# Adding the attention mask on VectorE and moving the softmax's subtraction to GpSimd in a two-layer transformer kernel

## Chip, cores and metric

The kernel runs on one core of a Trainium2 chip. The metric is the device time of the whole program in microseconds (us), the median of the runs. The engines are TensorE (PE, with its weight loads shown apart as PEld), VectorE (DVE), ScalarE (ACT), GpSimd (POOL) and SyncE (SP, which issues most DMAs). Each has a queue of its own that runs in order, and they wait for each other through semaphores.

## What is computed

Two layers, each of an attention part and a block part with modulation around them. The change is in the block part, `local_attention`, which is there twice: six blocks with 16 heads and a window of 32 in the first layer, two blocks with 8 heads and a window of 64 in the second; 4096 rows of 128 features in both. Cut to what matters:

```python
def local_attention(q, k, v):            # window w, keys of this window and the one before
    bk2, bv2 = look(bk), look(bv)
    mask = (it < jb) | (it > jb + w) | (jb == -1)
    sim = jnp.einsum('bhwie,bhwje->bhwij', bq, bk2) * QK_SCALE
    sim = jnp.where(mask, -jnp.finfo(sim.dtype).max, sim)
    attn = jax.nn.softmax(sim, -1)
    return jnp.einsum('bhwij,bhwje->bhwie', attn, bv2)
```

Around it stand the projection to q, k and v, an l2 norm with scales and rotary tables on q and k, the output projection, and a feed-forward part with a layer norm and a Gelu gate.

## The kernel before

`two_layer_kernel` runs a row of stages one after the other. The change touches `local_block_stage` alone, which is called twice: as `L0` (6 blocks, 16 heads, window 32), from about 1040 to 4560 us of the profiled span, and as `L1` (2 blocks, 8 heads, window 64), from about 4900 us to the end.

A stage takes the rows in tiles of 128, 16 tiles to a sequence of 2048 rows, two sequences to a block. A counter `k` goes over block and sequence (`HL` = 12 passes in L0, 4 in L1), `T` over the 16 tiles. Each tile is worked in two halves, `hf` 0 and 1, each with half of the heads. Everything is pipelined by hand: in step (T, hf) each engine's `emit` works on items that lag by a fixed number of halves: projection 4, values and normed keys 6, scores 7 (`AT_SCORE`), softmax 8 (`AT_SOFTMAX`), weighted values 9 (`AT_PV`), output transposes 10. In the feed-forward part two tiles form a group: even T does the up projection (`TO_UP`) in hf 0 and the layer norm's work (`TO_LN`), odd T the feature transposes and the down projection in hf 0. Thus four kinds of half alternate: up half (hf 0, even T), even output half (hf 1, even T), down half (hf 0, odd T), odd output half (hf 1, odd T). DVE, ACT, POOL and SP unroll 16 tiles per loop turn (`bodies`); PE unrolls two tiles (`paired_bodies`), with a tile number that is partly in a register (`Tile`).

The order in each queue is that of `emit`:

- PE: query/key projection (L1437), transposes of q and k (L1472), transposes of the attended values (L1491), values (L1506), transposes of the probabilities (L1521), then up projections (L1612), or output (L1533) and input transpose (L1543), or feature transposes and down projection (L1597, L1624); then the scores: two bf16 mask products against an identity (L1556) that open the PSUM banks, and the score products (L1564) that add to them; last the weighted values (L1585 in L0, L1587 in L1). The Gelu's gate shares PSUM banks with the weighted values, so they wait for `hidden_done` in the up half.
- DVE: reciprocal (L1855) and scaling (L1860) of the weighted values, `shift`: the negated maximum of the scores (L1869) and its addition to them (L1874), both read from PSUM; then the rotation (L1889, L1890) with the sum of squares (L1891), `clamp` (L1900), `add_output` (L1908), or `gated` (L1939) and `deviations`, or `add_group` (L1950).
- ACT: squares (L1677), copies of the q/k transposes (L1688), output copy (L1696), in hf 0 `roots` (L1704, L1707); in the up half exponentials (L1729), value copy (L1722), probability copy (L1737), table load (L1791), Gelus (L1795), table load; in the other halves value copy, then (even output half) `normalised` (L1773), exponentials, probability copy. `affine` (L1785) ends the down half.
- POOL: in hf 0 `refine`, four small steps that wait for ACT's root (L1977 to L1983); in the even output half `deviation_refine`, seven small steps (L2021 to L2033); then `to_unit_length` (L1993), in hf 1 `scaled_table` (L2012), and `add_parts` (L2002).

The buffer `probs` takes the shifted scores; ACT's exponential works in place on it.

Of the kernel before, what the change touches and what calls it, by code (L numbers as in the profile page):

```python
# [13 lines left out]
ALU = mybir.AluOpType  # L14
# [1025 lines left out]
def local_block_stage(nc, name, depth, heads, window, x, x_rows, mid_rows, v_rows, weights, tables):  # L1040
# [18 lines left out]
    with ExitStack() as ctx:  # L1059
# [28 lines left out]
        probs = sb("probs", [128, 2, 512])  # L1088
        neg_max = sb("neg_max", [128, 2, 2 * HU])
# [47 lines left out]
            "ss_done", "rotated", "max_done", "shifted", "rec_done", "att_done", "clamped", "mid_done", "bn_stats", "bn_eps", "bn_aggr", "var_done",  # L1137
# [124 lines left out]
        with nc.Block() as block:  # L1262
# [161 lines left out]
            def _(pe):  # L1424
# [84 lines left out]
                def prob_transposes(k, T, hf):  # L1509

                    t, h = item(T, hf, AT_PV)
                    if live(k, t):
                        pe.wait_ge(v2_in[parity(t)][h], turns(k, t, 16 * V2_LOADS))
# [31 lines left out]
                def of_sequence(t):  # L1545

                    return ds((t.turn * 2 + t.step % NP) % NP, 1) if isinstance(t, Tile) else slice(t % NP, t % NP + 1)

                def scores(k, T, hf):

                    t, h = item(T, hf, AT_SCORE)
                    if live(k, t):
                        wait(pe, S["shifted"], halves(k, t, h - 1))
                        wait(pe, S["kprev_done"], count(k, t, 1, 0))
                        for p in range(2):
                            nc.tensor.matmul(S_VIEW[:, p, :, :], ident_bf[:, :], masks[:, of_sequence(t), :].to_broadcast([128, HU, 2 * W]), start=True, stop=False)  # L1556
                        pe.wait_ge(consts_in, CONSTS)
                        pe.wait_ge(S["qkT_done"], steps_(k, t, NS * h + NS - 1))
                        kk = 1 + parity(t)
                        for i in range(HU):  # L1560
                            for a in range(NB):
                                for p in range(2):
                                    rows, u = slice(64 * p, 64 * p + 64), HU * h + i
                                    last = nc.tensor.matmul(S_VIEW[W * a:W * a + W, p, i, :], qkT[rows, 0, u, W + W * a:2 * W + W * a],  # L1564
                                                            qkT[rows, kk, u, W * a:W * a + 2 * W], start=False, stop=(i == HU - 1))
# [270 lines left out]
            def _(dve):  # L1836
# [25 lines left out]
                def shift(k, T, hf):  # L1862

                    t, h = item(T, hf, AT_SOFTMAX)
                    if live(k, t):
                        wait(dve, S["shifted"], halves(k, t - 1, h))
                        dve.wait_ge(S["score_ps"], halves(k, t, h))
                        top = neg_max[:, h, :].rearrange("x (p u) -> x p u", p=2)
                        nc.vector.tensor_reduce(top, S_VIEW, AX.X, ALU.max, negate=True).then_inc(S["max_done"], 1)  # L1869
                        wait(dve, S["pT_ps"], halves(k, t - 1, h))  # L1870
                        dve.wait_ge(S["max_done"], halves(k, t, h))
                        dst = probs[:, h, :].rearrange("x (u p k) -> x p u k", u=HU, p=2)
# [96 lines left out]
            def _(pool):  # L1969
# [65 lines left out]
                def emit(k, T, hf):  # L2035
                    if hf == 0:
                        refine(k, T)
                    elif T % 2 == TO_LN % 2:
                        deviation_refine(k, T)
# [107 lines left out]
```

## Time and profile before

| | us |
|---|---|
| median of 3 runs | 5893.61 |
| range of the runs | 5891.54 to 5894.18 |
| profiled execution | 5897.42 |
| its span | 5895.6 |

| engine | busy us | share of the span |
|---|---|---|
| PE | 4715.3 | 80% |
| PE weight loads | 3408.2 | 58% |
| DVE | 4302.1 | 73% |
| ACT | 3151.1 | 53% |
| POOL | 2961.3 | 50% |

The granted TensorE clock is full (1.00) over both block stages apart from their ends; its mean over the span is 0.886. How to read it: the shares are means over stages of different kinds. In the two block stages each engine repeats the same order of instructions every two tiles, so one such turn, read in order of time, stands for the stage. A row of the timeline has the start, the duration, the engine, the line, the operation with output and input, and in brackets how long the engine was idle before it and what released it.

### The profile page before, as it was taken

The numbers are of one execution on the slowest core, as the hardware profiler recorded it, in microseconds if no ns is written. First come the engines' busy times: TensorE is split into PE (matmuls) and PEld (weight loads), VectorE is DVE, ScalarE is ACT, GpSimd is POOL, SyncE is SP. The second block draws the span as 40 slices with busy tenths as digits, with TensorE's granted clock in tenths as the row PEclk, the third lists the DMA queues.
The fourth block names the chain that finished last, engine by engine and source line by source line (L and its number), as shares of the span: only waits on it lengthen the run. The fifth ranks groups of instructions, "written<-read, shape, count | busy, mean of one in ns | idle before, by whom it ended". The sixth has DMA issues, their size and how long they took to land. (4 is left out here: it accounts for less than half of the span.)

```text
span 5895.6 us, 217646 instructions
## 1 busy us (share of the span) xinstructions
PE 4715.3 (80%) x78080; PEld 3408.2 (58%) x78080; DVE 4302.1 (73%) x9236; ACT 3151.1 (53%) x6761; POOL 2961.3 (50%) x4044
## 2 busy tenths in 40 slices
PE   2005675799999999999999999999993774888886
PEld 1004553566666666666666666666663553666665
DVE  5995677677777777777777777777775545766665
ACT  1000221466666666666666666666662121666665
POOL 0886000566666666666666666666661001545442
PEclk6555666899999999999999999999997556999998
DMA  1000000445444454455454545454541001333332
GB/s 65 0 0 1 25 21 26 127 125 131 132 129 132 128 135 127 131 130 135 124 138 124 134 127 135 123 138 122 137 125 39 0 0 50 108 109 106 104 109 76
DMA packets 708756, 564.14 MB, mean 96 GB/s; under 512 B 227460, under 2 KB 633704, under 8 KB 707848
## 3 DMA queue, kind: packets, MB, share of 16 engines
q1 hardware_dynamic: 694920, 537.26, 34.3%
q10 hardware_dynamic: 13312, 22.02, 1.2%
q14 instruction: 455, 3.73, 0.2%
q8 instruction: 69, 1.13, 0.1%
HBM read 359.55 MB, written 199.76 MB: 95 GB/s over the span
## 5 line engine op out<-in xcount | busy, mean ns | idle before, releaser
L2002 POOL TENSOR_TENSOR L_qk<-L_cos_part,L_sin_part 128x512 f32<-128x512 f32 x896 | 1128.7, 1274 | 187.0 <-DVE L_sin_part L1890 186.5
L1677 ACT ACTIVATE L_squares<-L_ps_q 128x512 f32<-128x512 f32 x896 | 535.0, 597 | 1074.1 <-PE L_ps_q L1437 1064.3
L1437 PE MATMUL L_ps_q<-L_w_qkv,L_xT 128*128 128x512 f32 x1792 | 975.1, 626 | 67.8 <-issue 51.4
L1993 POOL TENSOR_TENSOR L_qk<-L_qk,L_rnorm 128x1024 f32<-128x1024 f32 (+1 forms) x512 | 865.1, 1690 | 20.7 <-POOL L_rnorm L1983 1.1
L1472 PEld LDWEIGHTS L_ps_t<-L_ident,L_qk 128*128 128x128 f32 x3584 | 448.0, 141 | 478.3 <-issue 375.6
L1889 DVE TENSOR_TENSOR L_cos_part<-L_ps_q,L_rot 128x512 f32<-128x512 f32 x896 | 609.4, 680 | 46.2 <-POOL L_rot L2012 34.7
L1977 POOL TENSOR_TENSOR L_nw_a<-L_rnorm 128x32 f32<-128x32 f32 (+1 forms) x256 | 60.0, 234 | 1116.4 <-ACT L_rnorm L1707 1116.2
L1890 DVE TENSOR_TENSOR L_sin_part<-L_ps_q,L_rot 128x512 f32<-128x512 f32 x896 | 609.2, 680 | 0.0
L1891 DVE TENSOR_REDUCE L_sumsq<-L_squares 128x8 f32<-128x512 f32 x896 | 604.8, 675 | 0.0
L1472 PE MATMUL L_ps_t<-L_ident,L_qk 128*128 128x128 f32 x3584 | 540.6, 274 | 3.7 <-POOL L_qk L1993 3.6
L1506 PE MATMUL L_ps_t<-L_w_qkv,L_xT 128*128 128x512 f32 (+1 forms) x1024 | 479.9, 550 | 74.6 <-issue 72.9
L1688 ACT ACTIVATE L_qkT<-L_ps_t 128x512 f32<-128x512 f32 x896 | 530.0, 592 | 14.1 <-PE L_ps_t L1472 13.8
L1533 PE MATMUL L_ps_q<-L_w_out,L_outT 128*128 128x128 f32 x3584 | 443.7, 276 | 1.7 <-ACT L_outT L1696 1.7
L2012 POOL TENSOR_TENSOR L_rot<-L_rot_base,L_qk_scales 128x256 f32<-128x256 f32 x256 | 187.6, 733 | 509.8 <-DMA L_qk_scales<-in_L_ffn_k_scale 508.8
L1533 PEld LDWEIGHTS L_ps_q<-L_w_out,L_outT 128*128 128x128 f32 x3584 | 421.5, 192 | 2.3 <-issue 2.3
L1521 PEld LDWEIGHTS L_ps_t<-L_ident,L_probs 128*128 128x128 f32 x2048 | 224.1, 140 | 333.8 <-issue 258.0
L1564 PE MATMUL L_ps_s<-L_qkT 64*32 64x64 f32 (+1 forms) x26624 | 416.1, 229 | 0.0
L1874 DVE TENSOR_TENSOR L_probs<-L_ps_s,L_neg_max 128x512 f32<-128x512 f32 x512 | 354.1, 692 | 53.5 <-DVE L_neg_max L1869 0.5
L1855 DVE RECIPROCAL L_p_rec<-L_ps_o 128x8 f32<-128x8 f32 (+1 forms) x512 | 103.0, 201 | 392.7 <-PE L_ps_o L1585 265.4
L1564 PEld LDWEIGHTS L_ps_s<-L_qkT 64*32 64x32 f32 (+1 forms) x26624 | 322.9, 107 | 108.1 <-issue 108.1
L1585 PE MATMUL L_ps_o<-L_val,L_probsT 64*32 64x65 f32 x24576 | 330.7, 226 | 61.2 <-DVE L_hidden L1939 50.7
L1860 DVE TENSOR_TENSOR L_att<-L_ps_o,L_p_rec 128x512 f32<-128x512 f32 (+1 forms) x512 | 320.0, 625 | 60.7 <-DVE L_p_rec L1855 10.8
(295 smaller groups left out, 9734.4 us busy)
## 6 DMA issues: line engine op xcount, KB each, us to landing
L_val<-v_rows SPq DMA_DIRECT2D x896, 260.0 KB, 3.9
v_rows<-L_val SPq DMA_DIRECT2D x384, 260.0 KB, 2.3
v_rows<-L_val SPq DMA_DIRECT2D x512, 65.0 KB, 2.2
L_rot_base<-in_rot SPq DMA_DIRECT2D x256, 128.0 KB, 2.1
v_rows<-L_val SPq DMA_DIRECT2D x128, 130.0 KB, 2.1
L_x_in<-x_rows SPq DMA_DIRECT2D x512, 32.0 KB, 1.7
mid_rows<-z SPq DMA_DIRECT2D x256, 64.0 KB, 1.6
L_f_in<-mid_rows SPq DMA_DIRECT2D x256, 64.0 KB, 2.0
```

Source lines behind the costliest of these rows:

```text
L1437: nc.tensor.matmul(ps_q[j % 2][:, :], xT[:, parity(t), :], w_qkv[:, 0:2, 256 * j:256 * j + 256], start=True, stop=True).then_inc(S["proj_p ...
L1472: last = nc.tensor.transpose(ps_t[0][:, 128 * i:128 * i + 128], qk[:, parity(t), h, s, 128 * i:128 * i + 128], ident[:, :])
L1506: nc.tensor.matmul(ps_v[:, 0:128 * HU], xT[:, parity(t), :], w_qkv[:, 2, 128 * HU * h:128 * HU * h + 128 * HU], start=True, stop=True).the ...
L1533: last = nc.tensor.matmul(ps_q[0][:, 0:128], outT[:, u, :], w_out[:, u, :], start=(u == 0), stop=(u == U - 1))
L1564: last = nc.tensor.matmul(S_VIEW[W * a:W * a + W, p, i, :], qkT[rows, 0, u, W + W * a:2 * W + W * a], qkT[rows, kk, u, W * a:W * a + 2 * W ...
L1677: nc.scalar.activation(squares[:, j % 2, :], ps_q[j % 2][:, :], ACT.Square).then_inc(S["sq_done"], 1)
L1688: nc.scalar.activation(dst, ps_t[0][:, :].rearrange("x (a u q) -> x a u q", a=2, u=2), ACT.Copy).then_inc(S["qkT_done"], 1)
L1889: nc.vector.tensor_tensor(R4(cos_part[:, j % 2, :]), qkp, cs[:, :, 0, :, :, :].to_broadcast([128, 2, 4, 2, 32]), ALU.mult)
L1890: nc.vector.tensor_tensor(R4(sin_part[:, j % 2, :]), qkp[:, :, :, ::-1, :], cs[:, :, 1, :, :, :].to_broadcast([128, 2, 4, 2, 32]), ALU.mul ...
L1891: nc.vector.tensor_reduce(sumsq[:, t % 2, j, :], squares[:, j % 2, :].rearrange("x (g d) -> x g d", g=8), AX.X, ALU.add).then_inc(S["ss_do ...
L1993: nc.gpsimd.tensor_tensor(v, v, r, ALU.mult).then_inc(S["normed"], 1)
L2002: nc.gpsimd.tensor_tensor(qk[:, t % 2, h, s, :], cos_part[:, j % 2, :], sin_part[:, j % 2, :], ALU.add).then_inc(S["added"], 1)
```

## The change

The two mask products on PE go. Each score product now opens and closes its own accumulation. DVE's `shift` becomes `mask`: it adds the mask (bf16, broadcast over heads) to the scores while it reads them from PSUM, and writes to a new SBUF tile `masked`; the maximum is then taken from `masked`. The subtraction of the maximum moves to POOL, in a new `shift` that reads `masked` and writes `probs`; it stands in POOL's queue behind `refine` or `deviation_refine` and ahead of `to_unit_length`. DVE's `mask` waits for POOL's previous `shift`. PE no longer waits for `shifted` and for `kprev_done` ahead of the scores; in the loop, the wait for the buffer stands ahead of the probability transposes (`masked`).

```diff
@@ sb
         probs = sb("probs", [128, 2, 512])
+        masked = sb("masked", [128, 512])
@@ PE, prob_transposes
                     if live(k, t):
+                        if isinstance(T, Tile):
+                            last_scores, g = item(T, hf, AT_SOFTMAX)
+                            pe.wait_ge(S["masked"], halves(k, last_scores, g))
@@ PE, scores
-                        wait(pe, S["shifted"], halves(k, t, h - 1))
-                        wait(pe, S["kprev_done"], count(k, t, 1, 0))
-                        for p in range(2):
-                            nc.tensor.matmul(S_VIEW[:, p, :, :], ident_bf[:, :], masks[:, of_sequence(t), :].to_broadcast([128, HU, 2 * W]), start=True, stop=False)
+                        before, keys = halves(k, t, h - 1), steps_(k, t, NS * h + NS - 1)
                         pe.wait_ge(consts_in, CONSTS)
-                        pe.wait_ge(S["qkT_done"], steps_(k, t, NS * h + NS - 1))
+                        if not isinstance(T, Tile):
+                            wait(pe, S["masked"], before)
+                        pe.wait_ge(S["qkT_done"], keys)
...
-                                                            qkT[rows, kk, u, W * a:W * a + 2 * W], start=False, stop=(i == HU - 1))
+                                                            qkT[rows, kk, u, W * a:W * a + 2 * W], start=True, stop=True)
@@ DVE
-                def shift(k, T, hf):
+                def mask(k, T, hf):
 
                     t, h = item(T, hf, AT_SOFTMAX)
                     if live(k, t):
-                        wait(dve, S["shifted"], halves(k, t - 1, h))
+                        wait(dve, S["shifted"], halves(k, t, h - 1))
                         dve.wait_ge(S["score_ps"], halves(k, t, h))
-                        top = neg_max[:, h, :].rearrange("x (p u) -> x p u", p=2)
-                        nc.vector.tensor_reduce(top, S_VIEW, AX.X, ALU.max, negate=True).then_inc(S["max_done"], 1)
-                        wait(dve, S["pT_ps"], halves(k, t - 1, h))
-                        dve.wait_ge(S["max_done"], halves(k, t, h))
-                        dst = probs[:, h, :].rearrange("x (u p k) -> x p u k", u=HU, p=2)
-                        wide = neg_max[:, h, :].rearrange("x (p u o) -> x p u o", p=2, o=1).to_broadcast([128, 2, HU, 2 * W])
-                        nc.vector.tensor_tensor(dst, S_VIEW, wide, ALU.add).then_inc(S["shifted"], 1)
+                        allowed = masks[:, t % NP, :].rearrange("x (p u k) -> x p u k", p=1, u=1).to_broadcast([128, 2, HU, 2 * W])
+                        view = masked[:, :].rearrange("x (u p k) -> x p u k", u=HU, p=2)
+                        nc.vector.tensor_tensor(view, S_VIEW, allowed, ALU.add).then_inc(S["masked"], 1)
+                        dve.wait_ge(S["masked"], halves(k, t, h))
+                        top = neg_max[:, h, :].rearrange("x (u p) -> x u p", p=2)
+                        nc.vector.tensor_reduce(top, masked[:, :].rearrange("x (u p k) -> x u p k", u=HU, p=2), AX.X, ALU.max, negate=True).then_inc(S["max_done"], 1)
@@ POOL
+                def shift(k, T, hf):
+
+                    t, h = item(T, hf, AT_SOFTMAX)
+                    if live(k, t):
+                        wait(pool, S["pT_ps"], halves(k, t - 1, h))
+                        pool.wait_ge(S["max_done"], halves(k, t, h))
+                        wide = neg_max[:, h, :].rearrange("x (n o) -> x n o", o=1).to_broadcast([128, 2 * HU, 2 * W])
+                        nc.gpsimd.tensor_tensor(probs[:, h, :].rearrange("x (n k) -> x n k", k=2 * W), masked[:, :].rearrange("x (n k) -> x n k", k=2 * W), wide, ALU.add).then_inc(S["shifted"], 1)
@@ POOL, emit
                         deviation_refine(k, T)
+                    shift(k, T, hf)
                     to_unit_length(k, T, hf)
```

## Rows read from the trace of the kernel before

**Rows 1.** The page, busy us, share of the span and instructions of each engine.

```profile
PE 4715.3 (80%) x78080; PEld 3408.2 (58%) x78080; DVE 4302.1 (73%) x9236; ACT 3151.1 (53%) x6761; POOL 2961.3 (50%) x4044
```

**Rows 2.** The timeline, first stage's up half: start, duration, engine, line, tiles.

```profile
2911.61 0.69 DVE L1874 TENSOR_TENSOR L_probs<-L_ps_s,L_neg_max 128x512 f32<-128x512 f32 x1
2914.30 0.63 ACT L1729 ACTIVATE L_probs<-L_probs 128x512 f32<-128x512 f32 x1
2914.48 0.25 POOL L1983 TENSOR_TENSOR L_rnorm<-L_rnorm,L_nw_a 128x32 f32<-128x32 f32 x1
2914.81 1.90 POOL L1993 TENSOR_TENSOR L_qk<-L_qk,L_rnorm 128x1024 f32<-128x1024 f32 x1
2915.31 0.60 ACT L1737 ACTIVATE L_probsT<-L_ps_t 128x512 f32<-128x512 f32 x1
2915.93 1.28 ACT L1791 ACT_TABLE_LOAD   x1
2918.78 0.47 DVE L1939 SCALAR_TENSOR_TENSOR L_hidden<-L_ps_o,L_b_up,L_gate 85x256 f32<-85x256 f32 x1
2919.32 0.72 PEld L1585 LDWEIGHTS L_ps_o<-L_val,L_probsT 64*32 64x32 f32 x64 [0.69 <-issue]
```

**Rows 3.** The timeline, first stage's even output half.

```profile
2922.39 0.20 POOL L2033 TENSOR_TENSOR L_f_b<-L_f_b,L_minus_one 128x2 f32<-128x2 f32 x1
2925.63 0.62 ACT L1729 ACTIVATE L_probs<-L_probs 128x512 f32<-128x512 f32 x1
...
2926.32 1.28 POOL L2002 TENSOR_TENSOR L_qk<-L_cos_part,L_sin_part 128x512 f32<-128x512 f32 x1
2926.41 1.24 DVE L1900 TENSOR_TENSOR L_nw_x<-L_sumsq,L_tiny 128x32 f32<-128x32 f32 x1
2926.60 0.38 PE L1556 MATMUL L_ps_s<-L_masks,L_ident_bf 128*128 x2
2926.91 0.70 PEld L1564 LDWEIGHTS L_ps_s<-L_qkT 64*32 64x32 f32 x64 [0.21 <-issue]
2928.53 0.21 DVE L1855 RECIPROCAL L_p_rec<-L_ps_o 128x8 f32<-128x8 f32 x1 [0.68 <-PE L_ps_o L1585]
```

**Rows 4.** Groups by line, second stage: count, busy us, mean ns, idle before.

```profile
L2002 POOL TENSOR_TENSOR L_qk<-L_cos_part,L_sin_part 128x512 f32<-128x512 f32 x128 | 162.7, 1271 | 63.1 <-DVE L_sin_part L1890 63.1
L1993 POOL TENSOR_TENSOR L_qk<-L_qk,L_rnorm 128x512 f32<-128x512 f32 x128 | 133.6, 1044 | 5.7 <-POOL L_rnorm L1983 1.1
L1874 DVE TENSOR_TENSOR L_probs<-L_ps_s,L_neg_max 128x512 f32<-128x512 f32 x128 | 88.5, 692 | 13.6 <-DVE L_neg_max L1869 0.5
L1891 DVE TENSOR_REDUCE L_sumsq<-L_squares 128x8 f32<-128x512 f32 x128 | 86.4, 675 | 0.0
```

**Rows 5.** The timeline, second stage's up half.

```profile
5304.78 0.61 ACT L1729 ACTIVATE L_probs<-L_probs 128x512 f32<-128x512 f32 x1
5305.85 0.22 POOL L1983 TENSOR_TENSOR L_rnorm<-L_rnorm,L_nw_a 128x16 f32<-128x16 f32 x1
```

**Rows 6.** The timeline, first stage's down half.

```profile
2932.52 0.25 POOL L1983 TENSOR_TENSOR L_rnorm<-L_rnorm,L_nw_a 128x32 f32<-128x32 f32 x1
2933.12 0.62 ACT L1729 ACTIVATE L_probs<-L_probs 128x512 f32<-128x512 f32 x1
2933.64 0.59 ACT L1737 ACTIVATE L_probsT<-L_ps_t 128x512 f32<-128x512 f32 x1
2935.83 0.72 PEld L1585 LDWEIGHTS L_ps_o<-L_val,L_probsT 64*32 64x32 f32 x64
```

**Rows 7.** The timeline, second stage's down half.

```profile
5319.59 0.62 ACT L1729 ACTIVATE L_probs<-L_probs 128x512 f32<-128x512 f32 x1
5320.03 0.22 POOL L1983 TENSOR_TENSOR L_rnorm<-L_rnorm,L_nw_a 128x16 f32<-128x16 f32 x1
5320.11 0.59 ACT L1737 ACTIVATE L_probsT<-L_ps_t 128x512 f32<-128x512 f32 x1
5322.27 0.60 PEld L1587 LDWEIGHTS L_ps_o<-L_val,L_probsT 128*64 128x64 f32 x16 [0.17 <-issue]
```

**Rows 8.** Line L1900's own view: count, ns min/median/max, first and last start.

```profile
L1900 DVE TENSOR_TENSOR L_nw_x<-L_sumsq,L_tiny x256: 174/674/1324, 1058.8 to 5818.1; 128x32 f32<-128x32 f32 x96, 128x16 f32<-128x16 f32 x32
```

More of the change, by code:

```diff
@@ L1135, in local_block_stage @@
             "ln_log", "ln_root", "fnorm_done", "fT_done", "gelu_done",
-            "ss_done", "rotated", "max_done", "shifted", "rec_done", "att_done", "clamped", "mid_done", "bn_stats", "bn_eps", "bn_aggr", "var_done",
+            "ss_done", "rotated", "masked", "max_done", "shifted", "rec_done", "att_done", "clamped", "mid_done", "bn_stats", "bn_eps", "bn_aggr", "var_done",
             "hidden_done", "new_done",
@@ L1543, in input_transpose @@
                         nc.tensor.transpose(ps_v[:, 0:128], x_in[:, parity(t), :], ident[:, :]).then_inc(S["xT_ps"], 1)
-                def of_sequence(t):
-                    return ds((t.turn * 2 + t.step % NP) % NP, 1) if isinstance(t, Tile) else slice(t % NP, t % NP + 1)
                 def scores(k, T, hf):
@@ L1953, in emit @@
                     normalise(k, T, hf)
-                    shift(k, T, hf)
+                    mask(k, T, hf)
                     for s in range(NS):
```

## Prediction, made before the changed kernel was seen

> **What bounds the kernel now.** I read the page first. PE is busy for 80% of the span, DVE 73%, ACT 53%, POOL 50% [rows 1]: in a mean over all stages PE leads, and POOL looks as if it had room. But a share of the span says nothing of which wait ends last, so I went to the order of time in the middle of each block stage, half by half. A half is one call of each engine's `emit`; I measure from the end of one weighted-values product (L1585, L1587) to the end of the next. Four kinds alternate: the up half (hf 0, even T: up projections, Gelu), the even output half, the down half (hf 0, odd T: down projection), the odd output half. Two tiles are one turn of four halves: 12 x 8 = 96 turns in the first block stage, 4 x 8 = 32 in the second.
>
> In three kinds of half of the first stage PE sets the length: after the transposes of the probabilities it runs without a gap up to the weighted values. The mask product lies in that gapless stretch [rows 3]. The up half is different. There ACT works from the exponentials through the copy of the values, the copy of the transposed probabilities, the table load and the three Gelus with no gap; DVE's `hidden` follows, and PE's weighted values, whose PSUM bank the gate shares, start at 2919.32, behind `hidden` which ended at 2919.25; PE's weight loads stood idle for 0.69 us just before [rows 2]. The table load starts 2915.93, the exponentials stood at 2914.30. In this half ACT is the limit, and what ACT's queue waits for is what counts.
>
> **Mask products removed.** PE streams the mask from 2926.60, the product's row has 0.38 us, and the scores start at 2926.91, after 0.21 us of idle weight loads [rows 3]. Without the product the scores can start at 2926.60: 0.31 us for a half. The bounds are 0.21 (only that idle goes) and 0.38 (the whole row). The saving counts only where PE sets the half.
>
> **DVE.** Before: a maximum from PSUM and a subtraction from PSUM. After: an addition that reads PSUM and the bf16 mask, and a maximum from SBUF. The addition has the form of L1874, one operand from PSUM and one broadcast, 692 ns; the SBUF reduce has that of L1891, 675 ns [rows 4]. So DVE has the same load, and the maximum is done about when the subtraction is done now: its 0.68 us starts where L1874 starts, at 2911.61, so it ends at about 2912.29 in the up half [rows 2]. Nothing of DVE is on the path for that.
>
> **The subtraction on POOL: its price.** 512 elements with one broadcast operand on POOL: L1993 in the second stage is just that, 1044 ns. L2002, with two full operands, takes 1271 ns [rows 4]; that is the upper end, and I take 1.04 because the access patterns agree. It occurs 512 times, 535 us, which brings POOL from 50% to some 59%: no bound by load.
>
> The Trainium skill (GPSIMD Engine Reference, "Engine selection") advises against moving two-input elementwise work there and calls it about twice as slow as on VectorE. Twice 692 ns would be an estimate of 1.38 us; by it the forecast below would be 54 us higher (0.34 us in 160 halves). This trace's row for the same shape gives a factor of 1.5, and the sum goes by the row.
>
> **Its place in POOL's queue.** This decides. `shift` is emitted after `refine` (hf 0) or `deviation_refine`, and ahead of `to_unit_length`. In hf 0 `refine` waits for ACT's root of the same half, so the subtraction, whose input has been there since 2912.29, waits for a chain that it has nothing to do with. ACT's exponentials then wait for POOL, and behind them in ACT's queue stand, in the up half, the value copy, the probability copy, the table load and the Gelus. Everything now gapless moves.
>
> Up half, first stage: the chain's last operation ends at 2914.73 and POOL's next one starts at 2914.81; in that place the subtraction runs to 2915.85. A step from engine to engine costs 0.07 (`hidden` ends at 2919.25, PE follows at 2919.32), so ACT starts at 2915.92, where it starts at 2914.30 now [rows 2]. That is 1.62 us later, and `hidden` and the weighted values move by as much, since the stretch behind is rigid. The 0.31 saved on PE vanishes in a longer wait. Second stage: the chain ends at 5306.07, the subtraction at 5307.19, the exponentials start at 5307.26 instead of 5304.78: 2.48 us [rows 5].
>
> Down half, first stage: the chain ends at 2932.77, exponentials at 2933.96 instead of 2933.12, so 0.84 later; the probability copy ends at 2935.07 instead of 2934.23. The weighted values would start at 2935.83 - 0.31 = 2935.52 [rows 6]: 0.45 us to spare, and the 0.31 is kept. In the second stage this cover is too thin: chain end 5320.25, exponentials 5321.44 instead of 5319.59, 1.85 later; the probability copy then ends at 5322.55, the weighted values start at 5322.62 instead of 5322.27 [rows 7]: 0.35 us lost, nothing saved.
>
> Output halves: no `refine` there. In the even one POOL's seven small steps end at 2922.59 and the maximum at 2922.69, so the subtraction is done near 2923.8, and ACT comes to these exponentials only at 2925.63 [rows 3]: hidden, 0.31 kept. The odd one is the same in the first stage. In the second the late down half pushes DVE's sum and with it the maximum back; I let that half keep nothing, and bound it by 0.31 kept or lost.
>
> What else queues behind the subtraction on POOL: `to_unit_length` (PE's transposes of it come one half later), `scaled_table` and `add_parts` (DVE's rotation of the next half wants their buffers, behind four other DVE instructions). They move by 1 to 2 us, which I cost at nothing. No DMA is moved; the value stores of the up half leave later by what ACT's copy is late, and their readers come three halves on. PE's new wait for `masked` ahead of the probability transposes is met over 1 us early.
>
> **One cost of another kind.** DVE's `clamp` (L1900) takes the larger of two SBUF tiles. It took 1.24 us where POOL's L2002 was running beside it, the two ending at 2927.65 and 2927.60 [rows 3]; over the kernel it took 174 ns at least and 1324 at most [rows 8]. With POOL fuller it will wait nearly always. In this even output half DVE still idles 0.68 us before its next reciprocal [rows 3], so I cost it at nothing; if it misses a further POOL instruction, see the second rival. The rule behind it is in the Trainium skill (SBUF — State Buffer, "Who interferes with whom"): a DVE instruction with two SBUF inputs and a GpSimd instruction that reads SBUF exclude each other for a whole instruction. By that rule, the trace agrees (174 against 1324 ns), and the new mask addition, with one operand in PSUM, is free of it.
>
> **The sum.** First stage: 96 x 1.62 = +155.5 for up halves; 96 x 3 x 0.31 = -89.3 for the others. Second: 32 x (2.48 + 0.35 - 0.31 + 0) = +80.6. Together +146.8 us. The profiled execution took 5897.4 us, its span 5895.6, the median of the runs is 5893.6; all lie within 0.1%, so the sum is set on the median: 5893.6 + 146.8 = 6040 us, 2.5% slower. Bounds: POOL at 1.27 adds 0.23 x 160 = 37; the mask at 0.21 or 0.38 moves 320 halves, +32 or -22; the odd output half of the second stage, 10 either way.
>
> **Rivals.** (a) Faster than before: ACT's order turns out to have slack in the up half, because `refine` ends earlier once the kernel has settled, or the Gelus wait for PE's gate product and not for ACT. Then the up halves cost nothing and only the 320 savings and the second stage's 0.35 stand: 5893.6 - 99 + 11 = 5805 us. It decides where the subtraction ends before 2914.3. Against it: the table load starts 0.03 us after the copy, with no idle time [rows 2]. Chance 5%.
> (b) DVE becomes late through `clamp`: one further L2002, 1.27 us, in the even output half. `clamp` would end at 2928.92 with the sum `z` still behind it, and the next reciprocal, today at 2928.53, is wanted at 2928.22: about 1 us in each of 128 turns, +128: 6168 us. It is for the case that POOL's back-to-back instructions keep DVE out; against it, at 2926.41 DVE waited for one instruction only [rows 3]. Chance 8%.
> (c) The mask product was hidden beside the issue of the scores, the saving is nothing: 5893.6 + 155.5 + 32 x 2.83 = 6140. Chance 5%.
> (d) Part of the delay is given back later (ACT's idle time ahead of the next half's squares lets PE and ACT re-form), half of 236 us: about 5922. Chance 7%, of which a third within 0.2% or below.
>
> The forecast's mechanism holds 75%. The range 5975 to 6115 takes in the bounds and leaves out most of the rivals, about 2 in 10. A measurement of this kernel can tell 0.2% (12 us) from no change. Chances: faster 6%, same 2%, slower 92%.
>
> **What would show it.** Up halves longer by 1.6 and 2.5 us, POOL's new line between L1983's and L1993's counterparts there, ACT's exponentials idle before it with POOL as the releaser, some 1.5 us in the first stage's up halves and 0.8 in its down halves; PE's wait for `hidden` grown; output halves 0.3 us shorter; granted clock still full in these stages. It is wrong if the exponentials never wait for POOL, if POOL's line costs well over 1.27 us, or if `clamp` delays the next half.

## The result, and the profile after

The changed kernel takes 6035.86 us (median of 4 runs, 6029.47 to 6041.25) against 5893.9 us before (4 runs, 5891.54 to 5895.73): a ratio of 1.0241, with a 95% interval of 1.0223 to 1.0258. It is 142 us slower. The profiled execution took 6036.01 us, its span 6034.2 us.

First the page of the changed kernel: the busy time of the engines, and three of its groups (busy us, mean ns of one, idle time before and what ended it).

```profile
PE 4639.1 (77%) x77056; PEld 3313.0 (55%) x77056; DVE 4361.9 (72%) x9236; ACT 3157.4 (52%) x6761; POOL 3456.1 (57%) x4556
...
L1990 POOL TENSOR_TENSOR L_probs<-L_masked,L_neg_max 128x512 f32<-128x512 f32 x512 | 533.1, 1041 | 196.4 <-DVE L_neg_max L1872 191.5
...
L1728 ACT ACTIVATE L_probs<-L_probs 128x512 f32<-128x512 f32 x512 | 320.2, 625 | 316.7 <-POOL L_probs L1990 316.6
...
L1937 DVE SCALAR_TENSOR_TENSOR L_hidden<-L_ps_t,L_b_up,L_gate 128x256 f32<-128x256 f32 x256 | 112.1, 479 | 460.3 <-ACT L_gate L1794 439.1
```

PE has lost 76 us of work, POOL has gained 495 [rows 1], and neither is what the time went by. The second and third groups are: ACT was idle for 317 us ahead of the exponentials, all but 0.1 us of it released by POOL's subtraction, and DVE for 439 us behind the Gelus. By the medians of the wait (1.34 us in the first stage's up halves, 2.22 in the second's), some 200 of the 317 us stand in the up half; most of the rest stands in the down halves (0.58 and 1.58 us). The timeline of the changed kernel, first stage: the weighted values that end the odd output half, then the up half up to its own weighted values.

```profile
2972.53 0.85 PE L1584 MATMUL L_ps_o<-L_val,L_probsT 64*32 64x65 f32 x64
...
2975.12 0.69 DVE L1872 TENSOR_REDUCE L_neg_max<-L_masked 128x8 f32<-128x512 f32 x1
...
2978.05 0.25 POOL L1981 TENSOR_TENSOR L_rnorm<-L_rnorm,L_nw_a 128x32 f32<-128x32 f32 x1
...
2978.26 1.04 POOL L1990 TENSOR_TENSOR L_probs<-L_masked,L_neg_max 128x512 f32<-128x512 f32 x1
...
2979.34 0.63 ACT L1728 ACTIVATE L_probs<-L_probs 128x512 f32<-128x512 f32 x1 [1.34 <-POOL L_probs L1990]
...
2980.96 1.28 ACT L1790 ACT_TABLE_LOAD   x1
...
2980.99 1.13 PE L1611 MATMUL L_ps_t<-L_f_normT,L_w_up 128*128 128x256 f32 x4 [0.49 <-ACT L_probsT L1736]
...
2982.76 0.87 DVE L1937 SCALAR_TENSOR_TENSOR L_hidden<-L_ps_t,L_b_up,L_gate 128x256 f32<-128x256 f32 x2 [3.34 <-ACT L_gate L1794]
...
2984.13 0.85 PE L1584 MATMUL L_ps_o<-L_val,L_probsT 64*32 64x65 f32 x64 [1.22 <-DVE L_hidden L1937]
```

These rows answer to [rows 2]. The maximum is there at 2975.81, POOL takes the subtraction up at 2978.26, behind the last step of the chain, ACT's exponentials start 5.96 us after the previous weighted values ended (2979.34 - 2973.38) where they started at 4.50 before (2914.30 - 2909.80), and the half is 11.60 us long. A second engine feels the delay: PE's last up products (L1611) wait 0.49 us for ACT's copy of the probabilities, which they did not do before. They end at 2982.12, though, and `hidden` starts only at 2982.76, behind the first Gelu, so the Gelus still set the half's end. The next half, the even output half, of the same timeline; it answers to [rows 3]:

```profile
2991.22 1.24 DVE L1898 TENSOR_TENSOR L_nw_x<-L_sumsq,L_tiny 128x32 f32<-128x32 f32 x1
...
2991.48 0.70 PEld L1563 LDWEIGHTS L_ps_s<-L_qkT 64*32 64x32 f32 x64 [0.17 <-issue]
...
2992.14 0.85 PE L1584 MATMUL L_ps_o<-L_val,L_probsT 64*32 64x65 f32 x64
...
2993.09 0.21 DVE L1854 RECIPROCAL L_p_rec<-L_ps_o 128x8 f32<-128x8 f32 x1 [0.44 <-PE L_ps_o L1584]
```

It is 8.01 us long. Weight loads still stand idle for 0.17 us ahead of the scores, and DVE still has idle time behind its clamp. The second stage, up half and even output half:

```profile
5516.39 0.71 PE L1586 MATMUL L_ps_o<-L_val,L_probsT 128*64 128x65 f32 x16
...
5521.33 1.04 POOL L1990 TENSOR_TENSOR L_probs<-L_masked,L_neg_max 128x512 f32<-128x512 f32 x1
5522.40 0.63 ACT L1728 ACTIVATE L_probs<-L_probs 128x512 f32<-128x512 f32 x1 [2.22 <-POOL L_probs L1990]
...
5526.98 0.70 PE L1586 MATMUL L_ps_o<-L_val,L_probsT 128*64 128x65 f32 x16 [1.41 <-issue]
...
5532.92 0.70 PE L1586 MATMUL L_ps_o<-L_val,L_probsT 128*64 128x65 f32 x16 [0.25 <-issue]
```

Here ACT waits 2.22 us for POOL, and the up half takes 10.58 us (5527.68 - 5517.10).

One turn says little of the others, so I took from the timeline of each kernel all halves of both stages and the median length of each kind, from the end of one weighted-values product to the end of the next (90 to 93 halves of each kind in the first stage, 25 or 26 in the second; the others miss a record). The runs of the next section stand in the same table. U is the up half, N the even output half, F the down half, O the odd output half; a "turn" is the sum of the four means.

| kernel | U, N, F, O, first stage | turn | U, N, F, O, second stage | turn |
|---|---|---|---|---|
| before | 10.41, 8.22, 8.31, 8.24 | 35.28 | 8.44, 5.94, 6.75, 5.87 | 27.24 |
| after | 11.61, 8.00, 8.08, 8.15 | 36.04 | 10.53, 5.94, 6.95, 5.65 | 29.39 |
| e1_shift_first | 10.40, 8.00, 8.08, 8.13 | 34.70 | 8.64, 5.94, 6.54, 5.65 | 27.12 |
| e2_shift_late | 13.91, 8.00, 9.43, 8.22 | 40.11 | 12.12, 7.25, 8.06, 5.65 | 33.09 |
| e5b_act_plus3 | 10.43, 8.24, 8.30, 8.24 | 35.35 | 8.46, 5.94, 6.75, 5.87 | 27.29 |
| e7_before_exp_last | 10.41, 8.22, 8.32, 8.24 | 35.24 | 8.44, 5.94, 6.75, 5.87 | 27.28 |
| e3_exp_last | 10.40, 8.00, 8.08, 8.15 | 34.72 | 8.45, 5.94, 6.94, 5.66 | 27.30 |
| e6_both | 10.40, 8.00, 8.08, 8.15 | 34.72 | 8.44, 5.94, 6.54, 5.65 | 26.87 |
| e4_products_back | 11.62, 8.22, 8.30, 8.35 | 36.59 | 10.48, 5.94, 6.94, 5.86 | 29.55 |
| e9_all_dve | 10.41, 9.64, 8.08, 8.66 | 37.03 | 8.45, 5.93, 6.87, 5.66 | 27.42 |

From before to after the turns grow by 0.76 and 2.15 us: 96 x 0.76 + 32 x 2.15 = 142 us. That this is the measured difference to the microsecond is partly luck: for other kernels of the table the same sum is off by up to some 14 us. A direct count needs no mean. From the first to the last start of DVE's maximum (L1869 before, L1872 after) the first stage took 3388.3 us before and 3447.1 after, the second 846.0 and 927.1: 59 and 81 us more. Together that is 140 us, and the span grew by 139. Nothing is lost outside the two block stages, but the second has lost more than its turns show. The difference stands at its start. The first twelve halves, in which the feed-forward part hasn't set in and a half is short, took 66.2 us before and 84.5 after. First one such half of the changed kernel, then those twelve halves by the windows view, before and after (us of the window, busy and count of PE, PEld, DVE, ACT and POOL, granted clock, DMA share, GB/s):

```profile
5083.15 0.63 ACT L1728 ACTIVATE L_probs<-L_probs 128x512 f32<-128x512 f32 x1 [2.22 <-POOL L_probs L1990]
...
5084.64 0.71 PE L1586 MATMUL L_ps_o<-L_val,L_probsT 128*64 128x65 f32 x16 [2.53 <-issue]
```

```profile
4992.60:5058.80 66.20, 58.16 (x602) 40.56 (x603) 48.88 (x100) 39.43 (x98) 37.94 (x61) 0.98 0.43 116
```

```profile
5051.30:5135.80 84.50, 65.69 (x583) 44.91 (x582) 49.36 (x99) 40.48 (x99) 49.66 (x73) 0.85 0.36 95
```

Each of the six halves with hf 0 waits 1.5 to 2.2 us for POOL's subtraction there, PE stands still ahead of the weighted values (2.53 us in the row), and the granted clock of the stretch is 0.85 where it was 0.98, so PE was on the lower of its two levels for a part of it.

### The profile page after: what moved, and what is told of

It reads as the page before. It is cut to its first block and busy times, and to the rows that moved or that the text cites. A ratio compares the mean times of both kernels' runs of the same rounds, so it can differ in the third digit from the quotient of the medians.

```text
span 6034.2 us, 215298 instructions
## 1 busy us (share of the span) xinstructions
PE 4639.1 (77%) x77056; PEld 3313.0 (55%) x77056; DVE 4361.9 (72%) x9236; ACT 3157.4 (52%) x6761; POOL 3456.1 (57%) x4556
## 5 line engine op out<-in xcount | busy, mean ns | idle before, releaser
L2000 POOL TENSOR_TENSOR L_qk<-L_qk,L_rnorm 128x1024 f32<-128x1024 f32 (+1 forms) x512 | 863.9, 1687 | 0.2
L1990 POOL TENSOR_TENSOR L_probs<-L_masked,L_neg_max 128x512 f32<-128x512 f32 x512 | 533.1, 1041 | 196.4 <-DVE L_neg_max L1872 191.5
L1728 ACT ACTIVATE L_probs<-L_probs 128x512 f32<-128x512 f32 x512 | 320.2, 625 | 316.7 <-POOL L_probs L1990 316.6
L1937 DVE SCALAR_TENSOR_TENSOR L_hidden<-L_ps_t,L_b_up,L_gate 128x256 f32<-128x256 f32 x256 | 112.1, 479 | 460.3 <-ACT L_gate L1794 439.1
```

The costliest lines, as they stand in the source:

```text
L1990: nc.gpsimd.tensor_tensor(probs[:, h, :].rearrange("x (n k) -> x n k", k=2 * W), masked[:, :].rearrange("x (n k) -> x n k", k=2 * W), wide ...
L2000: nc.gpsimd.tensor_tensor(v, v, r, ALU.mult).then_inc(S["normed"], 1)
```

## The experiments

Two theories stood at the start. Mine: the loss is the subtraction's place in POOL's queue, behind a chain that waits for ACT, and it reaches the end through ACT's exponentials in the up half. The rival: the loss is the subtraction on POOL as such, a fuller engine, wherever it is put. Then, since the up half lost less than ACT was delayed, the question was how much slack it had; then, what the mask products had cost PE; and last, whether POOL was needed at all.

### The subtraction ahead of the chain

`e1_shift_first` is the changed kernel with one call moved in POOL's queue:

```diff
                 if hf == 0:
+                    shift(k, T, hf)
                     refine(k, T)
-                elif T % 2 == TO_LN % 2:
-                    deviation_refine(k, T)
-                shift(k, T, hf)
+                else:
+                    if T % 2 == TO_LN % 2:
+                        deviation_refine(k, T)
+                    shift(k, T, hf)
                 to_unit_length(k, T, hf)
```

> The changed kernel with one edit: in the halves with hf 0, POOL emits the subtraction ahead of refine instead of behind it; the other halves are as they were. Theory (the late exponentials are the whole loss): in the first stage's up half the maximum is done 2.43 us after the half's start, so the subtraction ends near 3.57 and the exponentials start where they did before the change (4.51); the up half falls from 11.61 to 10.41 us, the down half stays; 96 x 1.20 = 115 us back. In the second stage the exponentials start near 3.3 instead of 5.24, the up half falls by about 1.97 us, the down half by 0.3: 32 x 2.3 = 74 us back. About 5847 us, faster than the kernel before. Rival (POOL's added load, or clamp's waits for POOL, are the loss): the work on POOL is the same, so 6036 us within 15.

Measured: 5840.93 us (4 runs), 0.9909 of before, interval 0.9892 to 0.9925. The same instructions on the same engines, in another order on one of them, are 195 us faster than the changed kernel and 53 us faster than the one before. Its timeline, an up half of the first stage (the previous weighted values ended at 3020.09, 10.41 us before these do):

```profile
3022.60 1.04 POOL L1990 TENSOR_TENSOR L_probs<-L_masked,L_neg_max 128x512 f32<-128x512 f32 x1 [2.03 <-DVE L_neg_max L1872]
...
3024.60 0.63 ACT L1728 ACTIVATE L_probs<-L_probs 128x512 f32<-128x512 f32 x1
3024.77 0.25 POOL L1981 TENSOR_TENSOR L_rnorm<-L_rnorm,L_nw_a 128x32 f32<-128x32 f32 x1
...
3028.28 0.88 DVE L1937 SCALAR_TENSOR_TENSOR L_hidden<-L_ps_t,L_b_up,L_gate 128x256 f32<-128x256 f32 x2 [2.14 <-PE L_ps_t L1611]
...
3029.65 0.85 PE L1584 MATMUL L_ps_o<-L_val,L_probsT 64*32 64x65 f32 x64 [0.77 <-DVE L_hidden L1937]
```

POOL had been idle for 2.03 us when the maximum came; the subtraction is over before the chain's last step, and ACT's exponentials show no wait. The up half is back at 10.40 us. POOL's load is as in the changed kernel (3476.0 us busy against 3456.1), so the load costs next to nothing and the place nearly all. In the second stage the up half keeps 0.20 us (8.64): ACT is ready for the exponentials at 2.88 us in the median (from the previous weighted values), and the subtraction ends at 3.32. The slow start of the second stage is gone too: its first twelve halves take 66.6 us.

### The subtraction later still

`e2_shift_late`, again the changed kernel:

```diff
-                shift(k, T, hf)
                 to_unit_length(k, T, hf)
+                shift(k, T, hf)
```

> The changed kernel with one edit: POOL emits the subtraction behind to_unit_length in every half. This doubles the suspected wait. Theory (the late exponentials): they move by the 1.90 us (first stage) or 1.04 us (second) of to_unit_length. First stage: up half +1.9, down half +1.2 (the probability copy then ends after the scores), output halves 0: 96 x 3.1 = 298 us. Second stage: up and down halves +1.0 each, output halves +0.7 and +0.9: 32 x 3.6 = 116. About 6450 us. Rival (load of POOL or clamp): the order does not matter, 6036 us within 15.

Measured: 6536.35 us, one run, so without an interval. The rival fell once more: the work on POOL is the same, and the kernel is 500 us slower than the changed one. U grows to 13.91 and F to 9.43, in the second stage all but O. Counted as above, from the first to the last maximum, the first stage is 384 us longer than in the changed kernel where 298 was expected, the second 111 for 116: the 86 us above the expectation stand in the first stage. They are taken up at the end, with what the clock did.

### How much slack the up half had

In the changed kernel the exponentials of the first stage start 1.45 us later (median 5.96 after the previous weighted values, 4.51 before), yet the up half grew by 1.20. The group of `hidden` shows where 0.25 went. First the changed kernel, then the kernel before, from the groups by line in the window 1030 to 4600 us, the first stage (idle us before the group, and what ended it):

```profile
L1937 DVE SCALAR_TENSOR_TENSOR L_hidden<-L_ps_t,L_b_up,L_gate 128x256 f32<-128x256 f32 x192 | 84.1, 479 | 320.5 <-ACT L_gate L1794 308.9 <-PE L_ps_t L1611 11.6
```

```profile
L1939 DVE SCALAR_TENSOR_TENSOR L_hidden<-L_ps_t,L_b_up,L_gate 128x256 f32<-128x256 f32 x192 | 84.1, 480 | 195.6 <-PE L_ps_t L1612 172.1 <-ACT L_gate L1795 23.4
```

Before the change `hidden` waited for PE's up projection, not for ACT's Gelu. ACT's work was gapless in [rows 2], but the half went by PE. Two kernels without the change test that. `e7_before_exp_last` sends the exponentials behind the Gelus, to take them out of ACT's path:

```diff
                     if hf == 0 and T % 2 == TO_UP % 2:
-                        exponentials(k, T, hf)
                         val_copy(k, T, hf)
                         prob_copy(k, T, hf)
                         gates(k, T)
+                        exponentials(k, T, hf)
```

> The kernel before the change with one edit: in up halves ScalarE does the exponentials behind the Gelus and the second table load instead of ahead of the value copy. That takes 0.55 us out of the chain that the prediction called the limit of the up half. By the prediction (ScalarE is the limit there) 128 x 0.55 = 70 us faster, 5824. By the trace after (VectorE's first hidden product waited for PE's up products, 0.25 us later than for the Gelu) the up half stays: 5894 within 10.

Measured: 5894.97 us (10 runs), 0.9998, interval 0.9989 to 1.0008: no change, as the trace of after had it. Its timeline, up half of the first stage:

```profile
3017.69 0.60 ACT L1722 ACTIVATE L_val<-L_ps_t 128x512 f32<-128x512 f32 x1 [0.61 <-PE L_ps_t L1506]
...
3020.65 0.87 DVE L1939 SCALAR_TENSOR_TENSOR L_hidden<-L_ps_t,L_b_up,L_gate 128x256 f32<-128x256 f32 x2 [2.10 <-ACT L_gate L1795]
...
3022.01 0.85 PE L1585 MATMUL L_ps_o<-L_val,L_probsT 64*32 64x65 f32 x64 [0.55 <-DVE L_hidden L1939]
3022.59 0.63 ACT L1729 ACTIVATE L_probs<-L_probs 128x512 f32<-128x512 f32 x1
```

With the exponentials gone, ACT idles for 0.61 us until PE has the values ready: they had filled a gap. The median start of the Gelus moves from 7.44 to 7.35 only, and `hidden` does not move at all (8.19). So the edit didn't take 0.55 us out of ACT's path but 0.09, and as a test it is weaker than its expectation has it: if ACT were the limit, it would have given some 10 us, not 70. Against 10 us the measured interval (-6 to 5 us) says a little, and `hidden` standing still says more. That this row names a Gelu as the releaser is no proof against it: the second of the three Gelus ends at 7.35 + 2 x 0.40 = 8.15, just ahead of `hidden`, but `hidden` doesn't need it, for in the kernel before it starts at 8.19 with the second Gelu running to 8.24. The name is that of the event that came last. The other side, and the stronger test, is `e5b_act_plus3`, also from the kernel before, with three small copies added to ACT's queue (cut: the line that declares `spare`):

```diff
                     if hf == 0 and T % 2 == TO_UP % 2:
+                        for _i in range(3):
+                            nc.scalar.activation(spare[:, 2 * _i:2 * _i + 2], minus_half[:, :], ACT.Copy)
                         exponentials(k, T, hf)
```

> The kernel before the change with three small ScalarE copies (128x2, about 0.20 us each) ahead of the exponentials in the up halves. By the prediction's reading (in the up half ACT is the limit, no slack) 128 x 0.6 = 77 us: 5971. By the trace after, ScalarE's chain had 0.25 us of slack, because VectorE's first hidden product waited for PE's up products and not for the Gelu: 128 x 0.35 = 45 us: 5939.

Measured: 5907.09 us (10 runs), 1.002, interval 1.001 to 1.003. Both expectations were far too high, for one reason that has nothing to do with the question: the copies cost the queue 0.28 us, not the 0.6 I had taken. Its timeline:

```profile
3022.19 0.39 ACT L1810 ACTIVATE L_spare<-L_minus_half 128x2 f32<-128x2 f32 x3
3022.47 0.63 ACT L1730 ACTIVATE L_probs<-L_probs 128x512 f32<-128x512 f32 x1
```

and its group of `hidden` in the first stage:

```profile
L1942 DVE SCALAR_TENSOR_TENSOR L_hidden<-L_ps_t,L_b_up,L_gate 128x256 f32<-128x256 f32 x192 | 84.1, 479 | 205.8 <-ACT L_gate L1796 199.1 <-PE L_ps_t L1613 6.8
```

The exponentials start 0.28 us later (median 4.79), the Gelus 0.27 (7.71), `hidden` 0.03 (8.22), and its releaser is now the Gelu. So the slack was 0.25 us: of 0.28, 0.03 came through, and of 1.45 in the changed kernel, 1.20. By the turns' means (35.28 to 35.35, 27.24 to 27.29) the cost is 96 x 0.07 + 32 x 0.05 = 8 us, inside the measured interval of 6 to 18. Had ACT been the limit with no slack, the same 0.28 us would have cost 128 x 0.28 = 36 us, which that interval excludes.

### The exponentials out of the way

If the loss goes through ACT's exponentials, it can also be mended there, with POOL's queue left as the change has it. `e3_exp_last` is the changed kernel with the edit of `e7_before_exp_last`.

> The changed kernel with the same edit on ScalarE (exponentials last in up halves), POOL's order untouched. POOL's subtraction stays as late as it was, but nothing that the half's end needs queues behind the exponentials. Theory: the first stage's up half falls from 11.61 to 10.41 us, the second's from 10.53 to 8.44, the down halves keep their loss: 96 x 1.20 + 32 x 2.09 = 182 us back, 5854. If the loss came from POOL's load or from clamp: 6036 within 15.

Measured: 5857.14 us (4 runs), 0.9932, interval 0.9916 to 0.9949; the up halves are back at 10.40 and 8.45. An edit that is worth nothing in the kernel before is worth 179 us here. Against `e1_shift_first` 16 us are left: the down half of the second stage (6.94 against 6.54), whose exponentials the edit doesn't touch, and 10 us at the start of the second stage, whose first twelve halves take 76.3 us against 66.6. `e6_both` has both edits.

> Both cures in one kernel: POOL's subtraction ahead of refine in hf 0, and ScalarE's exponentials last in up halves. Against the first cure alone (5841) only the second stage's up half has something left to gain, 8.64 to 8.44 us, 32 x 0.2 = 6 us: 5835. Should the up half be limited by ScalarE, 128 x 0.5 more would go: 5775.

Measured: 5827.17 us (4 runs), 0.9882, interval 0.9866 to 0.9899. It is the fastest kernel of the study, 1.2% faster than the one before. It is also 14 us below `e1_shift_first`, where 6 were expected and the turns give 6; what the other 8 are was not looked into. The 5775 of the expectation proves nothing either way, since in `e7_before_exp_last` the edit moved the Gelus by 0.09 us and not by 0.5. Against before, by medians, it keeps the three savings on PE in the first stage and two in the second: 96 x (0.22 + 0.23 + 0.09) + 32 x (0.21 + 0.22) = 66 us, of 68 measured.

### The mask products put back

`e4_products_back` is the changed kernel with PE's two products in their old place, the DVE's addition kept:

```diff
+                        for p in range(2):
+                            nc.tensor.matmul(S_VIEW[:, p, :, :], ident_bf[:, :], masks[:, of_sequence(t), :].to_broadcast([128, HU, 2 * W]), start=True, stop=False)
...
-                                                            ..., start=True, stop=True)
+                                                            ..., start=False, stop=(i == HU - 1))
```

> The changed kernel with the two bf16 mask products put back on PE ahead of the scores, DVE's addition kept (the mask is added twice, which changes no weight). It prices the products alone. By the trace after, the scores start 0.22 us earlier without them in the first stage's output and down halves and the half gets shorter by 0.09 to 0.23; put back they should cost 96 x (0.22 + 0.23 + 0.15) + 32 x 0.2 = 64 us: about 6100 us. By the prediction's 0.31 us in 288 + 32 halves it would be 99 us, 6135. If the products are hidden (rival c), 6036 within 10.

Measured: 6106.04 us (4 runs), 1.0357, interval 1.034 to 1.0375: 70 us above the changed kernel. An even output half of its timeline:

```profile
3030.14 0.21 PEld L1562 LDWEIGHTS L_ps_s<-L_masks,L_ident_bf 128*128 128x128 bf16 x2
3030.24 0.38 PE L1562 MATMUL L_ps_s<-L_masks,L_ident_bf 128*128 x2
3030.55 0.70 PEld L1570 LDWEIGHTS L_ps_s<-L_qkT 64*32 64x32 f32 x64 [0.21 <-issue]
```

The rows look just as in [rows 3], product to scores 0.31 us; but the halves grow by 0.22 (N), 0.22 (F) and 0.20 (O), and by 0.21 in the second stage's O. The up half doesn't grow, nor does the second stage's N. 96 x 0.64 + 32 x 0.21 = 68 us. Without the product the weight loads stand idle for 0.17 us ahead of the scores anyway, so of the 0.31 between the two starts a part is not the product's.

### The subtraction back on DVE

The subtraction costs DVE 0.69 us, and the idle time ahead of `hidden` seemed to have room for it. `e9_all_dve` does it there, from `masked`, behind the maximum; POOL's queue is as before the change.

```diff
# DVE, mask(), behind the maximum; POOL's shift is removed
+                        wait(dve, S["pT_ps"], halves(k, t - 1, h))
+                        dve.wait_ge(S["max_done"], halves(k, t, h))
+                        nc.vector.tensor_tensor(probs[:, h, :]..., masked[:, :]..., wide, ALU.add).then_inc(S["shifted"], 1)
```

> The changed kernel with the subtraction on VectorE, reading masked and the maxima from SBUF; PE without mask products as in the change; POOL as before the change. VectorE has one more instruction of some 0.7 us in each half, with two SBUF inputs, so it may also wait for POOL. Theory: the exponentials come at 3.2 us or so, in time for every half, so no loss of the change's kind; but VectorE's stretch to its last instruction in the output halves grows from 7.6 to 8.3 us and passes the half's 8.0: +0.3 us in the first stage's 192 output halves against the first cure, about 5841 + 58 = 5900. If VectorE's load has room after all: 5841.

Measured: 6067.79 us (4 runs), 1.0296, interval 1.0279 to 1.0313. Neither came true. The timeline of an even output half of the first stage, then the line's own view (count, ns min, median, max):

```profile
3002.65 1.90 POOL L1995 TENSOR_TENSOR L_qk<-L_qk,L_rnorm 128x1024 f32<-128x1024 f32 x1
3002.85 2.25 DVE L1876 TENSOR_TENSOR L_probs<-L_masked,L_neg_max 128x512 f32<-128x512 f32 x1
...
3004.51 1.17 POOL L2014 TENSOR_TENSOR L_rot<-L_rot_base,L_qk_scales 128x256 f32<-128x256 f32 x1
...
3006.35 1.86 PEld L1537 LDWEIGHTS L_ps_q<-L_w_out,L_outT 128*128 128x128 f32 x16 [1.61 <-DVE L_sin_part L1892]
```

```profile
L1876 DVE TENSOR_TENSOR L_probs<-L_masked,L_neg_max x512: 691/692/2449, 1069.7 to 6005.3; 128x512 f32<-128x512 f32 x171
```

DVE's subtraction, with both inputs in SBUF, takes 692 ns in the median and 2.25 us in this row: it starts 0.20 us after POOL's `to_unit_length` and ends 0.55 us after it. The rotation behind it is late by that, PE's output product waits 1.61 us, and the half grows from 8.22 to 9.64. The old subtraction had its scores in PSUM and took 692 ns in the mean too [rows 4]. With the masked scores in SBUF it has the same price as work, but no longer runs freely beside POOL. By the Trainium skill (SBUF — State Buffer, "Who interferes with whom") a DVE instruction with two SBUF inputs and a GpSimd instruction that reads SBUF exclude each other, and the trace agrees (692 against 2449 ns). So once the masked scores are in SBUF, POOL is the better place for the subtraction: there the same subtraction, in the right place, is 227 us faster (5840.93 against 6067.79).

## Why the prediction was right, and where its steps were not

The forecast of 6040 us missed by 4 us, and the forecast's mechanism is the one that the runs show: the exponentials wait for a subtraction that stands behind a foreign chain, and the up halves get longer by most of that wait. That the sum came so near is luck, because errors of single terms cancel. Against the medians of the table:

| term | predicted us | measured us |
|---|---|---|
| first stage, up half | +1.62 | +1.20 |
| first stage, N, F, O | -0.31 each | -0.22, -0.23, -0.09 |
| second stage, up half | +2.48 | +2.09 |
| second stage, N | -0.31 | 0.00 |
| second stage, F | +0.35 | +0.20 |
| second stage, O | 0 | -0.22 |

**The delay of the exponentials: mis-sized by 0.17 and 0.12.** I predicted 1.62 and 2.48; the medians are 1.45 (4.51 to 5.96) and 2.36 (2.88 to 5.24). I had put 0.08 us between the chain's last step and the subtraction, which was the start of L1993 behind the chain in [rows 2]; but L1993 needs the chain's result and the subtraction doesn't. It starts 0.04 us before the chain's step ends (2978.26 against 2978.30). The step to ACT took 0.04 where I took 0.07.

**"In this half ACT is the limit": wrong.** It had 0.25 us of slack. I read from a stretch without gaps [rows 2] that it sets the pace, and didn't look at who released `hidden`, which was PE. Rival (a) was right that there was slack, but not by its path: the Gelus waited for nobody before the change (1.2 us of idle time ahead of all 288 in the first stage); it was `hidden` that waited, for PE's last up products. With 0.25 us against a delay of 1.45 and 2.36 the slack decided nothing. `e5b_act_plus3` (0.03 of 0.28) shows it, and `e7_before_exp_last` (no gain) agrees.

**Mask products: mis-sized, 0.22 for 0.31.** My lower bound of 0.21 was the truth. `e4_products_back` shows it from the other side. Rival (c), that the product was hidden, fell. Two halves differ. In the second stage's N the saving is nothing, because there the weighted values wait for ACT's copy of the probabilities: it ends at 5.13 in the median before and after, and PE starts at 5.23. I had not looked whether PE set that half. In the first stage's O it is 0.09: the transposes of the probabilities start at 4.13 instead of 4.03. The down half has the same step (4.22 for 4.11), yet its length gains 0.23; the even output half doesn't have it (4.01 in both). The new wait for `masked` stands ahead of these transposes, and I called it free; it may be what costs 0.10 here, but no kernel with the wait elsewhere was tried, so the cause stays open.

**Second stage, F and O.** In F the exponentials start at 5.03 for 3.34, the probability copy ends at 6.15 and the weighted values start at 6.25 for 6.02: cover and mechanism as predicted, 0.15 less of it. O kept its saving in full.

**The start of the second stage: put at nothing.** The prediction took all 32 turns of that stage as equal. The first twelve halves have no feed-forward work and are short, and all six halves with hf 0 wait, not only the up halves: they grew by 18.3 us, where three turns as measured later would have grown by 6. How much of it is the lower clock (0.85) wasn't separated. The sign "granted clock still full in these stages" failed here; elsewhere in both stages it held (1.00).

**POOL's price: right.** The subtraction took 1041 ns in the mean, by the shape of L1993 (1044) in [rows 4], and not the 1271 of two full operands. Against the 692 ns on DVE it is a factor of 1.5; the Trainium skill's factor of about 2 for two-input operations (GPSIMD Engine Reference, "Engine selection") is by the trace too much for this form. POOL rose to 57%, not 59: its busy time grew by 495 us and not by 535, since its back-to-back rows overlap by some hundredths (the subtraction ends at 2979.30, L2000 starts at 2979.26), and the span is longer.

**The clamp: cost nothing, and rival (b) fell.** It does wait nearly always now, as I said it would. The line's own view in the changed kernel answers to [rows 8]:

```profile
L1898 DVE TENSOR_TENSOR L_nw_x<-L_sumsq,L_tiny x256: 192/1240/1315, 1058.8 to 5955.1; 128x32 f32<-128x32 f32 x96, 128x16 f32<-128x16 f32 x32
```

The median rose from 674 to 1240 ns, the maximum stayed: DVE misses one instruction of POOL and not two, and the 0.44 us of idle time behind it in the output half above is what is left of 0.68 [rows 3].

**Nothing is given back.** Rival (d), half of the delay made up in later halves, fell: N and F are shorter by PE's saving alone.

With the terms as measured (medians), the sum is 96 x 0.66 + 32 x 2.07 = 130 us, and the start of the second stage adds 12. Stage by stage, from the first to the last maximum, the first was predicted at 66 us and has 59, the second at 81 and has 81; the second is met only because the start stands in for turns that were put too high.

## What to carry to other kernels

When an operation moves to another engine, its time is the smaller part of its price: ask what the instruction just ahead of it in the new queue waits for, since here one line's place was worth 195 us and the engine's extra 495 us of work next to nothing. Look at the start of a stage as well as its middle: twelve halves there lost 18 us where twelve halves of the second stage's middle lose 6. A stretch without gaps is not yet the limit; look at who releases the step behind it, and remember that the second to arrive isn't shown. And before two operands are put in SBUF for VectorE, look at what GpSimd does at that moment.

## What the runs showed of the hardware

**The clock in the latest placement.** In `e2_shift_late` the exponentials' delay by POOL leaves PE standing still for some 2.5 us and, soon after, 1.2 us in each up half of the first stage. Its timeline, the first row from the turn before that of the other two, and two rows of the windows view: us of the window, busy (and count) of PE, PEld, DVE, ACT and POOL, granted clock, DMA share, GB/s.

```profile
3001.33 1.17 PE L1584 MATMUL L_ps_o<-L_val,L_probsT 64*32 64x65 f32 x64 [0.64 <-issue]
...
3037.79 1.13 PE L1611 MATMUL L_ps_t<-L_f_normT,L_w_up 128*128 128x256 f32 x4 [2.46 <-ACT L_probsT L1736]
...
3040.92 0.85 PE L1584 MATMUL L_ps_o<-L_val,L_probsT 64*32 64x65 f32 x64 [1.21 <-DVE L_hidden L1937]
```

```profile
3001.30:3002.50 1.20, 1.17 (x65) 1.04 (x65) 0.73 (x6) 1.19 (x3) 0.00 (x0) 0.56 0.90 226
3000.00:3200.00 200.00, 172.80 (x3413) 121.57 (x3398) 140.17 (x280) 124.93 (x256) 130.83 (x165) 0.97 0.44 114
```

The first weighted-values product took 1.17 us at a granted clock of 0.56, near the lower of the two levels (1.2 GHz, 0.50 of 2.4), and the same product 0.85 us in the last row. The changed kernel has 1.00 over the same 200 us:

```profile
3000.00:3200.00 200.00, 183.95 (x3663) 130.04 (x3658) 155.76 (x294) 133.50 (x273) 144.58 (x181) 1.00 0.50 130
```

Of the 381 such products that the trace has whole in this stage, 54 took 1.0 us or more in `e2_shift_late` (up to 1.19), most of them in up halves; in the changed kernel it is 1 of 377. The up half grew by 2.30 us over the changed kernel where the exponentials moved by 1.98 (5.96 to 7.94): the weighted values start 1.99 us later (12.74 for 10.75), and the rest is the product itself, 1.05 us in the median of the up halves for 0.85. Of the 86 us above the expectation, all in the first stage, the medians put 96 x 0.40 = 38 in the up half and 96 x 0.15 = 14 in the down half (9.43 for 8.08, where 1.2 was expected); how much of them is the clock's was not separated.

**Smaller things.** POOL's L2014 took 1.17 us in the row of `e9_all_dve` where it overlapped DVE's two-input subtraction, where its median over that kernel is 735 ns. Three ACT copies of 128x2, which the trace records as 0.39 us in all, delayed the queue by 0.28.
